# First attention of a four-layer transformer stack: the mask's bias moves from TensorE's accumulation to a VectorE addition

## The reference, cut to what matters

```python
scores = jnp.einsum('bhsk,bhtk->bhst', q, k) / jnp.sqrt(jnp.float32(DK))
scores = jnp.where(mask[:, None, :, :], scores, NEG_INF)
attn = jax.nn.softmax(scores, axis=-1)
out = jnp.einsum('bhst,bhtv->bhsv', attn, v)
```

## Time and profile before

| what | us |
|---|---|
| median of 3 runs | 742.88 (742.69 to 750.19) |
| the profiled execution, whole | 743.47 |
| its span, first to last instruction | 741.6 |
| first attention, scores of tile 0 to the last logits | about 22.9 to 234.5 |
| one turn of its loop | 12.64 to 12.99 |

### The profile page before, as it was taken

How to read it: one execution, slowest core, us unless ns; L and a number is a source line. 1 busy time by engine, 2 the same in 40 slices (tenths; PEclk the granted TensorE clock), 3 DMA queues, 4 the chain that set the end, 5 groups by cost and what they waited for, 6 DMA issues and landing times.

```text
span 741.6 us, 14125 instructions
## 1 busy us (share of the span) xinstructions
PE 610.3 (82%) x5391; PEld 409.7 (55%) x5391; DVE 450.0 (61%) x1243; ACT 321.1 (43%) x698; POOL 216.0 (29%) x407
## 2 busy tenths in 40 slices
PE   4999999999995797553788899988888888846687
PEld 4576666666654585421455555555565555524674
DVE  3576768777775115779983565447656667275552
ACT  2453544445333242434431322206657677713164
POOL 2124242453444246300211405412523411020400
PEclk9999999999997798657697699999979999977898
DMA  8770000000002152000001132122030300030001
GB/s 257 187 233 1 1 1 1 1 16 1 8 8 76 47 167 80 0 1 0 0 1 35 29 89 64 36 57 64 6 96 5 98 6 7 4 114 1 3 0 58
DMA packets 33604, 34.51 MB, mean 47 GB/s; under 512 B 8730, under 2 KB 29506, under 8 KB 32962
## 3 DMA queue, kind: packets, MB, share of 16 engines
q1 hardware_dynamic: 31072, 31.02, 14.7%
q0 software_dynamic: 1024, 2.11, 0.8%
q10 hardware_dynamic: 1442, 0.48, 0.3%
HBM read 19.63 MB, written 5.26 MB: 34 GB/s over the span
## 4 chain that ended last, share of the span: by engine, by line
PE 62%; DVE 16%; issue 10%; ACT 4%; POOL 4%; DMA 3%; POOLq 0%; SPq 0%; DVEq 0%; ACTq 0%
PE bank L592 6%; PE bank L1676 6%; PE bank L1926 5%; PE bank L517 4%; PE bank L548 4%; PE bank L526 4%; PE bank L1941 3%; PE bank L1730 3%; PE bank L560 2%; PE bank L1974 2%; PE bank L2355 2%; PE bank L535 2%; DVE mx L2077 2%; POOL y_tokens L1224 2%; PE bank L446 2%
## 5 line engine op out<-in xcount | busy, mean ns | idle before, releaser
L2077 DVE TENSOR_REDUCE mx<-bank 128x4 f32<-128x512 f32 (+1 forms) x128 | 71.0, 581 | 40.4 <-PE bank L1934 40.1
L2145 ACT ACTIVATE area_a<-bank 128x512 f32<-128x512 f32 (+1 forms) x128 | 73.7, 597 | 38.4 <-PE bank L1941 37.0
L943 ACT ACTIVATE area_a<-bank,beta 128x154 f32<-128x154 f32 x128 | 41.9, 412 | 76.3 <-PE bank L517 76.0
L592 PEld LDWEIGHTS bank<-area_a 128*128 128x128 f32 x384 | 48.2, 196 | 24.7 <-issue 15.0
L1031 POOL TENSOR_TENSOR area_a<-area_a,rs 128x512 f32<-128x512 f32 (+1 forms) x48 | 40.9, 879 | 48.8 <-DVE rs L751 48.8
L592 PE MATMUL bank<-area_a 128*128 128x128 f32 x384 | 55.0, 288 | 0.0
L1676 PE MATMUL bank<-area_a 128*128 128x512 f32 x80 | 42.8, 663 | 0.9 <-DVE X L1624 0.9
L548 PE MATMUL bank<-area_a,xnT 128*128 128x512 f32 (+1 forms) x96 | 41.6, 515 | 0.0
L517 PE MATMUL bank<-ctx_flat,area_a 128*128 128x154 f32 x256 | 41.6, 296 | 0.0
L1264 POOL TENSOR_TENSOR g_veps<-g_mv,eps 128x4 f32<-128x4 f32 x20 | 4.0, 202 | 128.1 <-DVE g_mv L1259 128.1
L517 PEld LDWEIGHTS bank<-ctx_flat,area_a 128*128 128x128 f32 x256 | 36.4, 190 | 7.9 <-issue 7.1
(11 more groups left out here) (358 smaller groups left out, 1479.7 us busy)
## 6 DMA issues: line engine op xcount, KB each, us to landing
area_a<-xn_area SPq DMA_DIRECT2D x48, 128.0 KB, 2.5
area_b<-in_w SPq DMA_DIRECT2D x16, 256.0 KB
f<-in_f SPq DMA_DIRECT2D x1, 2048.0 KB
area_a<-in_f SPq DMA_DIRECT2D x1, 2048.0 KB, 8.5
area_b<-xn_area SPq DMA_DIRECT2D x6, 308.0 KB, 5.6
area_a<-in_rows SPq DMA_DIRECT2D x10, 128.0 KB, 2.8
x_slots<-xn_area SPq DMA_DIRECT2D x1, 1032.0 KB, 8.0
area_a<-x_slots SPq DMA_DIRECT2D x8, 129.0 KB
```

The lines of the kernel that those rows point to most:

```text
L592: m = pe.matmul(WO, eT0[:, i, :], vv0[:, b % 2, i, :], start=(i == 0), stop=(i == 11))
L943: m = act.activation(kk0[:, g % 2, h, :], src[:, (h - lo) * 2 * T:(h - lo + 1) * 2 * T], ACT.Identity, bias=beta0[:, h:h + 1])
L2077: dve.tensor_reduce(mx3[:, b % 2, aux, heads3(half, 1 - odd)], SCORES_RING3[j % 2][:, 0:4 * n].rearrange("p (h k) -> p h k", k=n), AX.X, A ...
L2145: act.activation((ea3 if aux else em3)[:, heads3(half, odd), :], EXP_RING3[j % 2][0:T if aux else 128, :].rearrange("p (h q) -> p h q", q= ...
```

## The change: one matmul fewer per piece, one addition more, and maxima and subtraction in SBUF

In `scores` the three matmuls of L547 go; the scores' matmul starts the accumulation itself. In `softmax` DVE now adds the bias to each piece as it moves it from PSUM into the SBUF tile of probabilities, waits for its own last addition, takes the three maxima from SBUF, and subtracts in place. TensorE no longer waits for GpSimd's bias (`pool_ready`), DVE does. The semaphore that lets TensorE overwrite the score banks is still the one counted by the subtractions.

```diff
--- before.py
+++ after.py
@@ -544,9 +544,8 @@
                     lo, hi = HEADS0[c]
                     t0, t1 = SLOTS0[c]
                     n, w = hi - lo, t1 - t0
-                    pe.matmul(S0[c][:, 0:n * w], ident_b[:, :], mask_bias[:, b:b + 1, t0:t1].to_broadcast([128, n, w]), start=True, stop=False)
                     pe.matmul(S0[c][:, 0:n * w], xnT[:, b % 2, :], kk0[:, b // 2 % 2, lo:hi, (b % 2) * T + t0:(b % 2) * T + t1],
-                              start=False, stop=True).then_inc(scores_in_psum, 1)
+                              start=True, stop=True).then_inc(scores_in_psum, 1)
@@ -654,7 +653,6 @@
             pe.wait_ge(prep0_dve_done, 4)
-            pe.wait_ge(pool_ready, 3)
             pe.wait_ge(const_loaded, 3 * 16)
@@ -726,17 +724,21 @@
             def softmax(b):
-                dve.wait_ge(scores_in_psum, 3 * b + 1)
-                dve.tensor_reduce(mshort0[:, :], shifted_to(b, 2)[0], AX.X, ALU.max)
+                for k, c in enumerate((2, 0, 1)):
+                    sc, e, n, w = shifted_to(b, c)
+                    t0, t1 = SLOTS0[c]
+                    dve.wait_ge(scores_in_psum, 3 * b + k + 1)
+                    m = dve.tensor_tensor(e, sc, mask_bias[:, b:b + 1, t0:t1].to_broadcast([128, n, w]), ALU.add)
+                linked(dve, m)
+                dve.tensor_reduce(mshort0[:, :], probs0(b, 2), AX.X, ALU.max)
                 for c in range(2):
                     lo, hi = HEADS0[c]
-                    dve.wait_ge(scores_in_psum, 3 * b + c + 2)
-                    m = dve.tensor_reduce(mlong0[:, lo:hi], shifted_to(b, c)[0], AX.X, ALU.max)
+                    m = dve.tensor_reduce(mlong0[:, lo:hi], probs0(b, c), AX.X, ALU.max)
                 linked(dve, m)
                 linked(dve, dve.tensor_tensor(mx0[:, :], mlong0[:, :], mshort0[:, :], ALU.max))
                 for c, (lo, hi) in enumerate(HEADS0):
                     sc, e, n, w = shifted_to(b, c)
-                    dve.tensor_tensor(e, sc, mx0[:, lo:hi].unsqueeze(2).to_broadcast([128, n, w]), ALU.subtract).then_inc(shifted_done, 1)
+                    dve.tensor_tensor(e, e, mx0[:, lo:hi].unsqueeze(2).to_broadcast([128, n, w]), ALU.subtract).then_inc(shifted_done, 1)
@@ -849,7 +851,7 @@
-            dve.wait_ge(pool_ready, 2)
+            dve.wait_ge(pool_ready, 3)
```

## The result

| kernel | median, us | lowest to highest | ratio of the runs to those of before, 95% interval |
|---|---|---|---|
| before | 742.97 (4 runs) | 742.69 to 750.19 | |
| changed | 770.64 (4 runs) | 769.81 to 773.94 | 1.0322 [1.0254, 1.0391] |

The change costs 27.7 us by the medians. The profiled execution of the changed kernel took 769.81 us, 26.3 more than that of before. Two stretches make up most of it. 13.3 us lie in the first attention, where the forecast had put them. 10.5 us lie behind it, in layers that the change does not touch. The experiments will show that VectorE's additions are not needed for such a loss: a mere delay of these layers is followed by one as large.

The account below looks back on a forecast made before the run. TensorE was taken as the bound, DVE's chain to `xn` right behind. Attention terms of 12.8 us plus 7.5 for the clock made 20.3 on the profiled 743.5, 763.8 there; 763 us against the median of 742.9, range 752 to 771.

Parts of the forecast that it names:

- The bound: First attention's loop: TensorE bounds, DVE's chain to `xn` right behind; what counts is which arrives last at L576.
- `xn` at TensorE in a heavy turn: At L576, `xn` comes 9.47 us after the turn's start, TensorE at 7.71, so TensorE stands 1.76 us.
- six heavy turns: First attention: six heavy tiles each 1.23 us longer through later `xn`, 7.4 us together.
- turn of tile 9, without the clock: Seventh heavy tile, starting at 135.80: `xn` at 10.11 instead of 8.49 us, so +1.6 us.
- six light turns: First attention: TensorE gives up all of its 0.53 us in standing; the tiles gain and lose nothing.
- turn of tile 14: End of the loop: path from scores to `xn` gets an addition and two maxima longer, less 0.53: +1.1 us.
- turn of tile 0: Ahead of the loop, L669 waits for DVE's bias behind the softmax and sums of tile 0: +1.1 us.
- tile 15, up to L572: End of the loop: DVE is heavy there and the whole delay shows, +1.6 us.
- one idle time in front of L575: Sign in a heavy tile's profile after: TensorE idle 1.7 to 1.8 us there, put down to `xn`.
- one of my signs of being wrong: Standing turning up in front of another line, such as the exponentials' readers, would mean the wrong chain was followed.
- The step that was mis-sized: the clock: TensorE's clock falls after standings, 1.5 us each; ten cost 0 to 15 us, half taken: 7.5 us.
- a plain shift: Behind the first attention's loop all work follows in series and only shifts, with no added term.

Follow-up runs that it names:

- DVE's half alone: The changed kernel with the mask's matmuls put back on TensorE, so the bias is added twice; median 771.56 us, ratio to before 1.0258.
- the last set of 17 runs: The kernel before, unedited, timed beside the last three kernels of the experiments; median 751.71 us.

## Why the prediction was right, and where it was right by luck

**The bound.** That the change is decided at TensorE's wait for `xn` is shown from both sides: DVE's half alone gives the same 13.95 us, and moving `xn` out from behind the softmax, with the norm for the experts and ACT's copies, gives 12.48.

**The terms of the attention.**

| term | forecast, us | measured |
|---|---|---|
| `xn` at TensorE in a heavy turn | 9.47 | 9.46 |
| six heavy turns | +7.4 | +7.5 |
| turn of tile 9, without the clock | +1.6 | +1.6 (14.58 in DVE's half alone, no fall) |
| six light turns | 0 | +0.7 |
| turn of tile 14 | +1.1 | +1.2 |
| turn of tile 0 | +1.1 | +0.9 |
| tile 15, up to L572 | +1.6 | +1.6 |

The light turns came out 0.1 us long each, and tile 1 0.3. The sizes of the additions and of the instructions moved to SBUF were those of the rows chosen: 684, 676 and 688 ns. The Trainium skill ("VectorE: DVE Perf Modes", the section on the TRN2 errata) has fixed parts of 58 cycles from SBUF and 120 from PSUM. The difference of 62 cycles would make the instructions from SBUF 65 ns shorter at its 0.96 GHz, an estimate, and does not show: 676 against 685 ns, and 688 against 686. Tile 15 is read only up to L572, since a fall of the clock lies behind it in the changed kernel and another later in the first profile of before; its standing was for DVE's norm (L766), not for ACT's copy as the forecast had it.

**Where it stood.** The forecast put one idle time in front of L575. There are two, and the first is at L572, for a result that I had not followed. A standing in front of another line was one of my signs of being wrong; here it is the same chain, since L766 and L718 both stand behind the softmax on DVE's list. The sum was right, the rows to expect were not.

**The step that was mis-sized: the clock.** Of the ten standings priced, two brought a fall, in both profiles of the changed kernel. In tile 9, 16.05 less the 14.58 of the same turn without a fall are 1.5 us. In tile 15 the clock is 0.53 for 3.30 us behind L572, 1.6 us more at full load. So the price of one was right, and the count of five was three too many. The fall that the first profile of before had behind its 1.68 us is missing in the changed kernel (1.00), which takes one off again: against that profile the term of 7.5 us came to about 1.6. The six heavy turns, with 1.3 us of visible idle each, kept 1.00, and so did that of tile 14, where 1.60 and 0.67 us of idle show in front of L572 and L575. That the falls come from standings is borne out by the twelve profiles taken together; which standing is followed by one is not explained. The rule of the Trainium skill ("TensorE: Matmul & The Clock Gate", the section on a second failure mode) is borne out behind two of the ten standings and not behind the others.

**What made up for it.** With the clock's term as measured the forecast would have been 757 us, and the median is 770.6, 0.4 us inside the upper end of the range. Most of the missing part is behind the attention (10.5 us) and ahead of tile 0 (1.7 us; in the kernel before the scores of tile 0 started at 22.88 in one profile and at 24.47 in the other). I held the later layers to be a plain shift. They are not: their time in the profiles of all kernels lies between 530.0 and 541.7 us with the same instructions. That the total landed in the range is partly luck: one term was too large and one was missing. The direction, and 15 us of the size, are the attention's and were read correctly.

**Open.** The runs show that the later layers' clock varies between executions of one kernel, and that a pure shift of 16.4 us is enough to lengthen them in all four runs seen. That agrees with 10 of the 11 totals of the changed kernel being at 768.5 us or above and only one at 762.5. They don't show what selects the form, nor why the kernel before was seen about equally often in a lower group and a higher one (in the last set of 17 runs, 8 between 742.2 and 745.3 us and 9 between 751.7 and 757.2).

## What to carry to other kernels

Work taken off the full engine is worth only what the next chain leaves over. Find the instruction at which the full engine meets it, and count on that chain: here 0.44 us of spare time stood against 1.57 us of additions, while DVE's busy share, 69 to 81% of a turn, promised room. The same additions cost almost nothing once the small result that TensorE waits for stood ahead of the rest of the softmax in DVE's list, behind the additions.

Judge such a change by the stretch that it touches, not by the total: the stretch repeated within 0.1 us and the totals of the kernel before spread over 15. The total has the last word all the same: a delay of 16.4 us, made of matmuls alone, cost 30 by the medians.

## What was not expected of the hardware

TensorE's granted clock in the later layers is not the same in each execution of a program. The kernel before took 530.3 us from tile 15 to the end at a mean granted clock of 0.87, and 538.1 at 0.83. Put 16.4 us later by matmuls alone, it took 541.7 at 0.83. In the attention, one standing (1.29 and 0.67 us of idle at tile 9) was followed by a stretch of 3.4 us at 0.58, while six shorter ones (0.6 and 0.66) and a longer one at tile 14 (1.60 and 0.67) left it at 1.00. In DVE's half alone it was tile 14 (1.58 and 0.67) that was followed by a fall, and tile 9 (0.83 and 0.66) was not. A standing of 1.68 us behind the loop was followed by 0.54 in one profile of the kernel before and by 1.00 in the next. The length of a standing alone does not tell whether the clock falls.
